# Norms of queries and keys summed in four quarters of the array, with square buffers kept for four chunks

## The chip, the cores and the metric

The kernel runs on one core of a Trainium2 chip. The metric is the device time of one execution in microseconds, as the median of several runs. The engines have an instruction stream each: TensorE (PE) multiplies matrices into PSUM, VectorE (DVE), ScalarE (ACT) and GpSimd (POOL) work on tiles, and SyncE (SP) and POOL issue DMA transfers. They wait for each other by semaphores only.

## What is computed

One layer over 4096 tokens of width 256: a layer norm, self-attention with 16 heads of 16, a shared expert and eight routed experts (two chosen for each token), all added to the input.

```python
xn = _layernorm(x)                                     # 4096 x 256
q, k, v = xn @ Wq.T, xn @ Wk.T, xn @ Wv.T              # 16 heads of 16
attn = softmax(einsum('bqhd,bkhd->bhqk', q, k) / 16)
att = einsum('bhqk,bkhd->bqhd', attn, v)
scores = softmax(xn @ gate_w.T); top 2 of scores + gate_b -> rw
h = silu((xn @ w1 + b1) * (xn @ w3 + b3))              # eight experts, width 352
x + att + sum_e rw * (h @ w2 + b2) + the shared expert
```

The softmax doesn't look for the largest energy of each row. It takes |q| max|k| as a bound: an exponent of q.k minus |q| max|k| is never positive. So the kernel needs |q| of each token and head and the largest |k| of each head. The product minus |q| max|k|, split into a high and a low part, is "the shift": two more rows of the contraction of each score matmul.

## The kernel before

**Two parts.** The front (0 to some 101 us) makes the layer norm, the projections of queries, keys and values, the norms and the shifts. The main loop (from the first score matmul to the end) goes over 16 heads and two sweeps of 2048 queries: PE makes scores (L863), ACT takes the exponential (L1157), PE multiplies by the values (L876), and the experts' matmuls (L888, L900) are woven in. The order of all instructions is written out by hand in each engine's function; nothing is planned by a scheduler.

**The front on PE.** Tokens go by eight chunks of 512 (`c`, NCH = 8, FIRST = 4). `turn_xn(c)` turns a chunk (L671), `keys(c, i)` and `queries(c, i)` project it with six matmuls of 128x512 each (L695, L696, L699), `late_queries` does so for chunks 4 to 7 at the end, and `value_rows(n)` makes values of two tiles with twelve matmuls (L764 to L766). ACT copies each projection out of PSUM and makes its squares in bf16 (`split_keys` L1057 and L1058, `split_queries` L1072 and L1073), and DVE takes the low part (`key_rest` L1322, `query_rest` L1329).

**The norms.** `key_norms(c)` (L727) and `query_norms(c)` (L736) sum the squares of one chunk over the 16 columns of each head: two matmuls of 128x128 with 512 moving columns, whose stationary operand is a slice of `hones_b` that puts the sums of chunk c on PSUM rows 16c to 16c+15. One buffer `sq` holds the squares of one chunk of keys and one of queries; ACT waits for the norms of chunk c-1 (`s_nk`, `s_nq`) before it writes those of chunk c. Keys add up in bank 7, queries of chunks 0 to 3 in rows 0 to 63 of bank 6, and those of 4 to 7 in rows 64 to 127 of bank 5.

**From norms to scores.** DVE reduces bank 7 (L1382), PE turns it (L803), DVE takes the largest per head (L1385), PE spreads it (L808), ACT takes the root (L1126). Then DVE makes the shifts of the first half of the queries from `qnorm` (`shift_rows(0)`, L1398 and L1400, 64 rows of 512), POOL stores them to DRAM (`store_shift`, L432, two transfers of 64 rows, 128 KB each), waits until both have landed (`s_sst[0]`), and loads the rows of head 0 into `q_ring` (`load_q_shift`, L424, four transfers that raise `s_qfirst`). PE's first score matmul waits for `s_qfirst` and for ACT's copies of the values (`s_vc`, L1081). The second half (queries 4 to 7) is made by L1133, `shift_rows(1)` and a store on SP. ACT's seventh exponential waits for both stores, because `qnorm` and `spart` lie in the buffer of `probs`.

**Queues.** POOL's transfers go by queue q0 of the DMA engines, those of SP by q1, where the stores of keys and queries are (`store_keys` L482, `store_queries` L489, 512 KB each).

Of the kernel before, what the change touches and what calls it, by code (L numbers as in the profile page):

```python
# [5 lines left out]
T = 4096  # L6
D = 256
# [138 lines left out]
def layer_program(nc, x, wqT, wkT, wvT, gT, gate_b, w1, w3, w2, b13, b2, ident, hones, prefix, ones, steps_c, out):  # L146
# [11 lines left out]
    with ctx:  # L158
# [7 lines left out]
        qshift_parts = nc.dram_tensor("qshift_parts", (NP_, H, T), f32, kind="Internal").ap()  # L166
# [7 lines left out]
        hones_b = sb("hones_b", [P, DT, 2 * P - H], bf16)  # L174
# [20 lines left out]
        o_n = sb("o_n", [P, NB_, HD], f32)  # L195
# [3 lines left out]
        zeros = sb("zeros", [P, TPU * D], f32)  # L199
        places_sb = sb("places_sb", [P, 3 * NT * E], f32)  # L200
# [47 lines left out]
        sq = pflat[:, 2048:3072].bitcast(bf16).rearrange("p (w i n) -> p w i n", w=2, i=DT)  # L248
# [170 lines left out]
        def load_q_shift(queue, h, sweep, landed):  # L419

            for r in range(2):
                for i in range(2):
                    dst = q_ring[r * HALF + SHIFT:r * HALF + SHIFT + NP_, sweep, i * QC:(i + 1) * QC].bitcast(f32)
                    queue.dma_start(dst, shift_cols[:, ds(h, 1), sweep, :, i, r, :].rearrange("s h c n -> (s h) c n")).then_inc(landed, 16)  # L424

        def store_shift(queue, half):

            rows = slice(half * HALF, (half + 1) * HALF)
# [9 lines left out]
        def _(sp):  # L438
# [71 lines left out]
            with sp.If(flag):  # L510
# [19 lines left out]
                for n in range(NCH):  # L530
                    sp.wait_ge(s_shift, n + 1)
                    sp.dma_start(qshift_parts[:, :, n * QC:(n + 1) * QC].rearrange("s h t -> h s t"), spart[0:H].bitcast(f32)).then_inc(s_gst, 16)
# [110 lines left out]
        def _(pe):  # L643
# [78 lines left out]
            def key_norms(c):  # L722

                pe.wait_ge(s_sq, key_job(c) + DT)
                own = slice(P - H - H * c, 2 * P - H - H * c)
                for dt in range(DT):
                    last = pe.matmul(bank(7), hones_b[:, dt, own], sq[:, 1, dt, :],  # L727
                                     start=(c == 0 and dt == 0), stop=(c == NCH - 1 and dt == DT - 1))
                last.then_inc(s_nk, 1)

            def query_norms(c):

                pe.wait_ge(s_sq, query_job(c) + DT)
                own = slice(P - H - H * c, 2 * P - H - H * c)
                for dt in range(DT):
                    last = pe.matmul(bank(6 if c < FIRST else 5), hones_b[:, dt, own], sq[:, 0, dt, :],  # L736
# [1074 lines left out]
```

## Time and profile before

| | us |
|---|---|
| median of 3 runs (lowest to highest) | 2132.31 (2130.73 to 2132.53) |
| the profiled execution, its own time | 2134.93 |
| its span | 2132.9 |
| PE busy | 2111.6 (99%) |
| ACT busy | 2016.2 (95%) |
| DVE busy | 805.7 (38%) |
| granted TensorE clock, as a share of full | 0.998 |

The span is the time from the first to the last instruction of the profiled execution; 2.0 us of its own time lie around it, and the median of the runs is 2.6 us below that time. Busy shares are means over two parts with different limits. Rows of the timeline give the start, the duration, the engine and line, and in brackets the idle time before the instruction and what ended it.

### The profile page before, as it was taken

The page shows a single profiled execution, that of the slowest core. Times are in us where ns is not written, and L with a number is a line of the kernel's source. Part 1 is how long each engine was busy: PE and PEld are TensorE (multiplying, and loading weights), DVE is VectorE, ACT ScalarE, POOL GpSimd, SP SyncE. Part 2 cuts the span into 40 slices and gives each one's busy share as a digit, 9 for nine tenths or more (in the row PEclk, how much of TensorE's full clock was granted, in tenths as well). Part 3 has the DMA queues.
Part 4 walks back from the last instruction along what each step waited for, and adds up shares of the span by engine and source line. Part 5 has one row for each costly group of instructions (what it writes and reads, how often), then busy time and mean ns, then how long its engine had stood idle before and what let it go on. Part 6 is the DMA issues. An engine that isn't in the chain of part 4 may idle for free.

```text
span 2132.9 us, 38290 instructions
## 1 busy us (share of the span) xinstructions
PE 2111.6 (99%) x15722; PEld 969.2 (45%) x15722; DVE 805.7 (38%) x1558; ACT 2016.2 (95%) x2228; POOL 253.5 (12%) x260
## 2 busy tenths in 40 slices
PE   8999999999999999999999999999999999999998
PEld 5734444444444444444444444444444444444442
DVE  7554333333333333333333333333333322244531
ACT  6699999999999999999999999999999999999998
POOL 0307764000000000000000000000000000122230
PEclk9999999999999999999999999999999999999999
DMA  8774433222231313132222221313122221322321
GB/s 284 263 251 126 125 123 100 60 53 72 58 79 51 76 52 82 51 78 60 64 59 72 63 75 51 87 44 79 51 79 59 71 68 57 85 80 86 105 91 41
DMA packets 223310, 187.28 MB, mean 88 GB/s; under 512 B 110623, under 2 KB 192342, under 8 KB 223134
## 3 DMA queue, kind: packets, MB, share of 16 engines
q1 hardware_dynamic: 209454, 148.68, 24.5%
q0 software_dynamic: 12624, 36.08, 5.2%
q8 instruction: 124, 2.03, 0.4%
q14 instruction: 52, 0.43, 0.1%
q10 hardware_dynamic: 1056, 0.07, 0.0%
HBM read 130.21 MB, written 54.53 MB: 87 GB/s over the span
## 4 chain that ended last, share of the span: by engine, by line
PE 95%; ACT 4%; DVE 1%; DMA 0%; issue 0%; SPq 0%; DVEq 0%; ACTq 0%
PE PS L876 44%; PE PS L863 31%; PE PS L888 12%; PE PS L900 6%; ACT probs L1157 3%; PE PS L695 0%; PE PS L696 0%; PE PS L699 0%; DMA hones_sb<-in_hones 0%; PE PS L764 0%; DVE probs L1303 0%; PE PS L671 0%; ACT x_parts L1038 0%; ACT x_full L1039 0%; PE PS L766 0%
## 5 line engine op out<-in xcount | busy, mean ns | idle before, releaser
L1157 ACT ACTIVATE probs<-PS 128x1024 f32<-128x1024 f32 x2048 | 1921.1, 1038 | 73.8 <-PE PS L863 45.1
L876 PE MATMUL PS<-probs,v_head 128*32 128x512 f32 x8192 | 989.9, 599 | 1.0 <-ACT probs L1157 0.8
L863 PE MATMUL PS<-q_ring,k_stack 50*128 50x512 f32 x4096 | 729.6, 443 | 5.7 <-ACT probs L1157 4.4
L863 PEld LDWEIGHTS PS<-q_ring,k_stack 50*128 50x128 f32 x4096 | 332.3, 184 | 607.4 <-ACT probs L1157 544.2
L876 PEld LDWEIGHTS PS<-probs,v_head 128*32 128x32 f32 x8192 | 211.4, 108 | 448.5 <-issue 372.9
L1598 DVE TENSOR_SCALAR gate_in<-PS,bias_sb 128x256 f32<-128x256 f32 (+7 forms) x165 | 76.4, 463 | 605.5 <-PE PS L888 597.0
L888 PE MATMUL PS<-x_hi,w_hi 128*128 128x256 f32 (+9 forms) x660 | 199.3, 302 | 0.0
L1227 POOL DMA_DIRECT2D slot_y<-y_sb x39 | 27.9, 716 | 1411.2 <-DVE y_sb L1668 1374.8
L888 PE MATMUL PS<-x_hi,w_lo 128*128 128x256 f32 (+9 forms) x660 | 184.9, 280 | 0.0
L888 PE MATMUL PS<-x_lo,w_hi 128*128 128x256 f32 (+9 forms) x660 | 184.2, 279 | 0.0
L888 PEld LDWEIGHTS PS<-x_hi,w_hi 128*128 128x128 f32 (+1 forms) x660 | 118.7, 180 | 53.2 <-issue 53.2
L888 PEld LDWEIGHTS PS<-x_lo,w_hi 128*128 128x128 f32 (+1 forms) x660 | 118.9, 180 | 0.0
L888 PEld LDWEIGHTS PS<-x_hi,w_lo 128*128 128x128 f32 (+1 forms) x660 | 118.9, 180 | 0.0
L1668 DVE COPY y_sb<-PS 128x512 f32<-128x512 f32 x39 | 27.0, 692 | 222.7 <-PE PS L900 222.7
L1608 DVE SCALAR_TENSOR_TENSOR hid<-hid,prod 128x768 f32<-128x768 f32 (+7 forms) x55 | 49.9, 908 | 130.1 <-ACT hid L1143 130.1
L900 PE MATMUL PS<-w_hi,hid_hi 128*128 128x256 f32 (+4 forms) x318 | 95.5, 300 | 0.0
L1629 DVE TENSOR_TENSOR w_lo<-w_raw,w_hi 128x1408 fp32r<-128x1408 f32 x55 | 89.2, 1622 | 1.6
L900 PE MATMUL PS<-w_lo,hid_hi 128*128 128x256 f32 (+4 forms) x318 | 89.6, 282 | 0.0
L900 PE MATMUL PS<-w_hi,hid_lo 128*128 128x256 f32 (+4 forms) x318 | 89.4, 281 | 0.0
L1218 POOL DMA_INDIRECT slot_x<-y_sb,pos x64 | 78.7, 1230 | 19.1 <-issue 14.0
L1603 DVE SCALAR_TENSOR_TENSOR prod<-PS,bias_sb,gate_in 128x256 f32<-128x256 f32 (+7 forms) x165 | 76.9, 466 | 5.9
L900 PEld LDWEIGHTS PS<-w_hi,hid_hi 128*128 128x128 f32 (+4 forms) x318 | 59.1, 186 | 13.4 <-issue 13.4
(186 smaller groups left out, 1148.7 us busy)
## 6 DMA issues: line engine op xcount, KB each, us to landing
w_raw<-in_w SPq DMA_DIRECT2D x110, 352.0 KB
k_stack<-qk_parts SPq DMA_DIRECT2D x120, 128.0 KB
w_raw<-in_w SPq DMA_DIRECT2D x55, 256.0 KB
q_ring<-qk_parts SPq DMA_DIRECT2D x372, 32.0 KB
qk_parts<-part_a SPq DMA_DIRECT2D x20, 512.0 KB, 4.3
slot_x<-zeros SPq DMA_DIRECT2D x39, 256.0 KB, 3.7
slot_in<-slot_x SPq DMA_DIRECT2D x156, 64.0 KB, 2.4
slot_y<-y_sb POOLq DMA_DIRECT2D x39, 256.0 KB, 2.5
```

The source lines that it names most:

```text
L863: last = pe.matmul(bank(2 * score_buffer(turn, g) + r), k_stack[rows, kt * P:(kt + 1) * P], q_ring[rows, sweep, i * QC:(i + 1) * QC], star ...
L876: last = pe.matmul(bank(O_BANK)[VW * j:VW * (j + 1), :], v_head[:, kt, :], probs[:, slot, (j % 2) * QC:(j % 2 + 1) * QC], start=(kt == 0), ...
L888: last = pe.matmul(f_half(w)[0:FT[j], 0:width(u)], a[u % 2][:, w, dt, j * P:j * P + FT[j]], b[:, dt * CH:dt * CH + width(u)], start=(n == ...
L900: last = pe.matmul(f_half(t)[0:own, :], a[0:rows, j, t * P:t * P + own], b[0:rows, j, :], start=(n == 0), stop=(n == 8))
L1157: nc.scalar.activation(probs[:, prob_slot(g), :], bank(2 * score_buffer(h, g), 2), ACT.Exp, scale=ENERGY_SCALE).then_inc(s_exp, 1)
L1218: nc.gpsimd.indirect_dma_start(out=slot_x, out_offset=bass.IndirectOffsetOnAxis(ap=pos[:, u * TPU + t, k:k + 1], axis=0), in_=rows[:, t, : ...
L1227: nc.gpsimd.dma_start(slot_y[(u - SA) * CH:(u - SA + 1) * CH, :].rearrange("(t p) d -> p t d", p=P), y_sb[:, u % 2, :].rearrange("p (t d) ...
L1598: V.tensor_scalar(gate_in[0:FT[j], 0:width(u)], f_half(0)[0:FT[j], 0:width(u)], bias_sb[0:FT[j], u % 2, j:j + 1], 0.5, ALU.add, ALU.mult). ...
L1603: V.scalar_tensor_tensor(prod[u % 2][0:FT[j], j, 0:width(u)], f_half(1)[0:FT[j], 0:width(u)], bias_sb[0:FT[j], u % 2, 3 + j:4 + j], gate_i ...
L1608: V.scalar_tensor_tensor(hid[:, :, 0:width(u)], hid[:, :, 0:width(u)], 1.0, prod[u % 2][:, :, 0:width(u)], ALU.add, ALU.mult).then_inc(s_h ...
L1629: V.tensor_tensor(w13_lo[u % 2][:, :, :, :], w13_raw[:, :, :, :], w13_hi[u % 2][:, :, :, :].bitcast(f32), ALU.subtract).then_inc(s_w13, 1)
L1668: V.tensor_copy(y_sb[:, u % 2, :], bank(F_BANK)).then_inc(s_yc, 1)
```

## The change

Buffers for the squares of four chunks of keys and four of queries replace `sq`. They lie in buffers that are free in the front (`o_t`, `x_t`, a part of `v_all`, and `early_sq`, into which `zeros`, `places_sb` and `o_n` are moved too). The norms are summed for four chunks at once: for each of the two halves of the width, four matmuls of 32 output columns, one for each chunk, to PSUM rows 32c to 32c+31. A half of a sequence has 16 valid rows in each quarter (keys of chunks 0 to 3 on the lower 16, of 4 to 7 on the upper 16 of each quarter, in one bank), the other 16 rows of a query bank are zero. So there are four blocks of eight matmuls in place of 16 pairs. ACT waits for norms twice in place of 14 times. `qnorm`, `spart` and the shift stores have 128 rows in place of 64 for each half (256 KB for each transfer), half of them zeros, and `load_q_shift` reads row sweep*H + h. Since both halves use the same rows of `qnorm` and `spart`, DVE takes the largest norm of the first half before its shifts (a new reduction), ACT's second root waits for the first shifts (`s_s1`), and `shift_rows(1)` waits for the first stores (`s_sst[0]`). POOL's `memset` of `zeros` waits for the last query norms.

```diff
-        hones_b = sb("hones_b", [P, DT, 2 * P - H], bf16)
+        hones_b = sb("hones_b", [P, DT, 3 * H], bf16)
...
-        sq = pflat[:, 2048:3072].bitcast(bf16).rearrange("p (w i n) -> p w i n", w=2, i=DT)
...
+        key_sq, query_sq = ([buf.bitcast(bf16).rearrange("p (i n) -> p i n", i=DT) for buf in bufs] for bufs in (
+            (pflat[:, 2048:2560], pflat[:, 2560:3072], o_t[:, :, :].rearrange("p b d -> p (b d)"), x_t[:, :]),
+            (early_sq[:, 0:QC], early_sq[:, QC:2 * QC], early_sq[:, 2 * QC:3 * QC], v_all[:, 22:24, :].rearrange("p t n -> p (t n)")[:, 0:QC])))
...
-                    queue.dma_start(dst, shift_cols[:, ds(h, 1), sweep, :, i, r, :].rearrange("s h c n -> (s h) c n")).then_inc(landed, 16)
+                    queue.dma_start(dst, shift_cols[:, ds(sweep * H + h, 1), sweep, :, i, r, :].rearrange("s h c n -> (s h) c n")).then_inc(landed, 16)
...
-                queue.dma_start(qshift_parts[s, :, cols].rearrange("h (c t) -> c h t", c=FIRST), spart[rows, s, :].bitcast(f32)).then_inc(s_sst[half], 16)
+                queue.dma_start(qshift_parts[s, :, cols].rearrange("h (c t) -> c h t", c=FIRST), spart[:, s, :].bitcast(f32)).then_inc(s_sst[half], 16)
...
+            def norms(w, half, b):
+
+                own = slice(0, 2 * H) if half else slice(H, 3 * H)
                 for dt in range(DT):
...
+                    for c in range(QCH):
+                        last = pe.matmul(bank(b)[2 * H * c:2 * H * (c + 1), :], hones_b[:, dt, own], (key_sq if w else query_sq)[c][:, dt, :],
+                                         start=((half == 0 or w == 0) and dt == 0), stop=((half == 1 or w == 0) and dt == DT - 1))
...
-            pe.wait_ge(s_hb, 2)
-            key_norms(0)
             for c in range(1, FIRST):
                 keys(c, 0)
-                query_norms(c - 1)
...
-                key_norms(c)
+                if c == FIRST - 1:
+                    pe.wait_ge(s_hb, 2)
+                    key_norms(0)
...
                 if c == FIRST:
-                    query_norms(FIRST - 1)
+                    query_norms(0)
...
-                key_norms(c)
+                if c == NCH - 1:
+                    key_norms(1)
...
-            query_norms(4)
...
-            query_norms(5)
...
-            query_norms(6)
...
-            query_norms(7)
+            query_norms(1)
...
-                if i == 0 and c:
-                    act.wait_ge(s_nq, c)
+                if i == 0 and c == FIRST:
+                    act.wait_ge(s_nq, 1)
...
+            act.wait_ge(s_nq, 2)
+            act.wait_ge(s_s1, NP_)
+            nc.scalar.activation(qnorm, bank(5), ACT.Sqrt).then_inc(s_qn, 1)
...
+            pool.wait_ge(s_nq, 2)
             nc.gpsimd.memset(zeros[:, :], 0.0).then_inc(s_zero, 1)
...
+                if half:
+                    dve.wait_ge(s_sst[0], 16 * NP_)
+                else:
+                    link(V.reduce_max(kmax[:, 3:4], qnorm, axis=AX))
+                V.tensor_scalar(spart[:, 0, :], qnorm, kmax[:, 2:3], None, ALU.mult).then_inc(s_s1, 1)
```

On PE, at the end of chunk 7 (the last key norms), the rows before are these; `probs` holds the squares:

```order
L766 MATMUL PS<-wvg_hi,x_parts 128x264
L727 MATMUL PS<-probs,hones_b 128x512 x2
L695 MATMUL PS<-x_parts,wqk_hi 128x512
L696 MATMUL PS<-x_parts,wqk_lo 128x512
L695 MATMUL PS<-x_parts,wqk_hi 128x512
```

and now, at the same place, the squares being in `probs`, `o_t` and `x_t`:

```order
L769 MATMUL PS<-wvg_hi,x_parts 128x264
L729 MATMUL PS<-probs,hones_b 32x512 x2
L729 MATMUL PS<-o_t,hones_b 32x512
L729 MATMUL PS<-x_t,hones_b 32x512
L729 MATMUL PS<-probs,hones_b 32x512 x2
L729 MATMUL PS<-o_t,hones_b 32x512
L729 MATMUL PS<-x_t,hones_b 32x512
L697 MATMUL PS<-x_parts,wqk_hi 128x512
```

Eight matmuls of 32 columns stand where a pair of 128 columns stood, and the pairs after chunks 4, 5 and 6 are gone.

On DVE, around the shifts of the first half, the rows before are

```order
L1329 TENSOR_TENSOR part_q<-PS,part_q 128x512 x2
L1392 TENSOR_SCALAR kmax<-kmax 128x1
L1398 TENSOR_SCALAR probs<-probs,kmax 64x512
L1400 SCALAR_TENSOR_TENSOR probs<-probs,kmax 64x512
L1329 TENSOR_TENSOR part_a<-PS,part_a 128x512 x4
```

and now

```order
L1331 TENSOR_TENSOR part_q<-PS,part_q 128x512 x2
L1394 TENSOR_SCALAR kmax<-kmax 128x1
L1402 TENSOR_REDUCE kmax<-probs 128x1
L1403 TENSOR_SCALAR probs<-probs,kmax 128x512
L1405 SCALAR_TENSOR_TENSOR probs<-probs,kmax 128x512
L1331 TENSOR_TENSOR part_a<-PS,part_a 128x512 x4
```

The reduction into `kmax` is new and stands ahead of both shift instructions, which have 128 rows; the low parts of chunks 6 and 7 follow as before.

## Rows read from the trace of the kernel before

**Rows 1.** Page: chain by engine, and the costliest group (busy us, mean ns | idle)

```profile
PE 95%; ACT 4%; DVE 1%; DMA 0%; issue 0%; SPq 0%; DVEq 0%; ACTq 0%
...
L1157 ACT ACTIVATE probs<-PS 128x1024 f32<-128x1024 f32 x2048 | 1921.1, 1038 | 73.8 <-PE PS L863 45.1
```

**Rows 2.** Chain of waits, in order of time: start us, us, engine and line

```profile
84.28 0.45 PE PS L736 x2
...
100.07 0.62 ACT v_all L1081
100.86 0.96 PE PS L863 x6
...
107.94 0.43 PE PS L863 x2
108.37 1.00 PE PS L876 x8
...
146.29 1.85 PE PS L876 x16
148.14 0.90 PE PS L863 x6
```

**Rows 3.** Timeline of PE in the front: start, us, line, shapes, [idle <-releaser]

```profile
1.46 6.55 PE L650 MATMUL PS<-o_t 128*128 128x512 bf16 x20 [1.46 <-DVE o_t L1273]
...
27.03 1.09 PE L671 MATMUL PS<-ident_sb,probs 128*128 128x128 f32 x8 [1.50 <-DVE probs L1303]
...
49.46 1.09 PE L671 MATMUL PS<-ident_sb,probs 128*128 128x128 f32 x8 [0.35 <-DVE probs L1303]
...
52.71 0.39 PE L764 MATMUL PS<-wvg_hi,x_parts 128*128 128x264 f32 x1 [0.30 <-ACT x_full L1039]
...
64.21 1.09 PE L671 MATMUL PS<-ident_sb,probs 128*128 128x128 f32 x8 [0.85 <-DVE probs L1303]
...
68.44 0.60 PE L727 MATMUL PS<-probs,hones_b 128*128 128x512 bf16 x2 [0.28 <-ACT probs L1058]
...
70.46 1.09 PE L671 MATMUL PS<-ident_sb,probs 128*128 128x128 f32 x8
...
74.69 0.60 PE L727 MATMUL PS<-probs,hones_b 128*128 128x512 bf16 x2 [0.28 <-ACT probs L1058]
...
94.46 0.61 PE L736 MATMUL PS<-probs,hones_b 128*128 128x512 bf16 x2
```

**Rows 4.** Timeline of DVE around chunk 7 and the shifts of the first half

```profile
69.03 1.37 DVE L1303 TENSOR_SCALAR probs<-resid,mv,rstd 128x256 f32<-128x256 f32 x4
...
88.08 0.48 DVE L1398 TENSOR_SCALAR probs<-probs,kmax 64x512 fp32r<-64x512 f32 x1
88.59 0.74 DVE L1400 SCALAR_TENSOR_TENSOR probs<-probs,kmax 64x512 fp32r<-64x512 f32 x1
...
95.91 0.69 DVE L1409 TENSOR_REDUCE qbound<-probs 128x1 f32<-128x512 f32 x1 [0.92 <-ACT probs L1133]
```

**Rows 5.** Timeline of POOL: the shift stores and the shift loads

```profile
88.85 1.41 POOL L432 DMA_DIRECT2D qshift_parts<-probs  x2 [3.22 <-DVE probs L1398]
95.55 2.20 POOL L424 DMA_DIRECT2D q_ring<-qshift_parts  x4 [5.29 <-DMA qshift_parts<-probs]
```

**Rows 6.** DMA issues at 88.8, 90 and 97.1 us: KB each, us to landing

```profile
qshift_parts<-probs POOLq DMA_DIRECT2D x1, 128.0 KB, 3.2
...
qshift_parts<-probs POOLq DMA_DIRECT2D x1, 128.0 KB, 5.6
...
q_ring<-qshift_parts POOLq DMA_DIRECT2D x2, 4.0 KB, 3.5
```

**Rows 7.** Window 81:91 (last: DMA share, GB/s); queues in 91:94: packets, MB, share

```profile
81.00:91.00 10.00, 10.00 (x45) 7.20 (x43) 5.14 (x10) 6.56 (x13) 5.93 (x12) 1.00 1.04 394
...
q1 hardware_dynamic: 354, 0.68, 61.1%
q0 software_dynamic: 246, 0.26, 40.2%
```

More of the change, by code:

```diff
@@ L198, in layer_program @@
         qbound = sb("qbound", [P, 2], f32)
-        zeros = sb("zeros", [P, TPU * D], f32)
-        places_sb = sb("places_sb", [P, 3 * NT * E], f32)
+        early_sq = sb("early_sq", [P, 3 * QC], f32)
         flag_f = sb("flag_f", [1, 4], f32)
@@ L720, in late_queries, with key_norms, query_norms @@
                 project(c, 0, i, late_bank(m))
-            def key_norms(c):
-                pe.wait_ge(s_sq, key_job(c) + DT)
-                own = slice(P - H - H * c, 2 * P - H - H * c)
+            def norms(w, half, b):
+                own = slice(0, 2 * H) if half else slice(H, 3 * H)
                 for dt in range(DT):
[L727 to L736, printed above, removed]
-                                     start=(c % FIRST == 0 and dt == 0), stop=(c % FIRST == FIRST - 1 and dt == DT - 1))
-                last.then_inc(s_nq, 1)
+                    for c in range(QCH):
+                        last = pe.matmul(bank(b)[2 * H * c:2 * H * (c + 1), :], hones_b[:, dt, own], (key_sq if w else query_sq)[c][:, dt, :],
+                                         start=((half == 0 or w == 0) and dt == 0), stop=((half == 1 or w == 0) and dt == DT - 1))
+                return last
+            def key_norms(half):
+                pe.wait_ge(s_sq, key_job((half + 1) * QCH - 1) + DT)
+                norms(1, half, 7).then_inc(s_nk, 1)
+            def query_norms(half):
+                pe.wait_ge(s_sq, query_job((half + 1) * QCH - 1) + DT)
+                norms(0, half, 6 - half).then_inc(s_nq, 1)
             def value_rows(n):
@@ L1057, in split_keys @@
                 nc.scalar.activation(key_part[c % 2][:, 0, i, :], bank(b), ACT.Copy).then_inc(s_hi, 1)
-                nc.scalar.activation(sq[:, 1, i, :], bank(b), ACT.Square).then_inc(s_sq, 1)
+                nc.scalar.activation(key_sq[c % QCH][:, i, :], bank(b), ACT.Square).then_inc(s_sq, 1)
             def split_queries(c, i):
@@ L1067, in split_queries @@
                     act.wait_ge(s_kst[0], stored(6))
-                if i == 0 and c:
-                    act.wait_ge(s_nq, c)
+                if i == 0 and c == FIRST:
+                    act.wait_ge(s_nq, 1)
                 b = 4 + i if c < FIRST else late_bank((c - FIRST) * DT + i)
@@ L1072, in split_queries @@
                 nc.scalar.activation(query_part[c][:, 0, i, :], bank(b), ACT.Copy).then_inc(s_hi, 1)
-                nc.scalar.activation(sq[:, 0, i, :], bank(b), ACT.Square).then_inc(s_sq, 1)
+                nc.scalar.activation(query_sq[c % QCH][:, i, :], bank(b), ACT.Square).then_inc(s_sq, 1)
             def keep_values(n):
@@ L1117, in _ @@
                     root(5)
-                    act.wait_ge(s_nq, FIRST)
-                    nc.scalar.activation(qnorm[0:HALF, :], bank(6)[0:HALF, :], ACT.Sqrt).then_inc(s_qn, 1)
+                    act.wait_ge(s_nq, 1)
+                    nc.scalar.activation(qnorm, bank(6), ACT.Sqrt).then_inc(s_qn, 1)
                 keep_values(c + 2)
@@ L1394, in shift_rows @@
             def shift_rows(half):
-                rows = slice(half * HALF, (half + 1) * HALF)
                 dve.wait_ge(s_qn, half + 1)
-                V.tensor_scalar(spart[rows, 0, :], qnorm[rows, :], kmax[rows, 2:3], None, ALU.mult).then_inc(s_s1, 1)
+                if half:
[3 more added lines that the diff above has]
+                V.tensor_scalar(spart[:, 0, :], qnorm, kmax[:, 2:3], None, ALU.mult).then_inc(s_s1, 1)
                 dve.wait_ge(s_s1, NP_ * half + 1)
-                V.scalar_tensor_tensor(spart[rows, 1, :], qnorm[rows, :], kmax[rows, 2:3], spart[rows, 0, :].bitcast(f32),
+                V.scalar_tensor_tensor(spart[:, 1, :], qnorm, kmax[:, 2:3], spart[:, 0, :].bitcast(f32),
                                        ALU.mult, ALU.subtract).then_inc(s_s1, 1)
@@ L1422, in _ @@
                 dve.wait_ge(s_tr, NCH)
-                dve.wait_ge(s_nk, NCH)
+                dve.wait_ge(s_nk, 2)
                 dve.wait_ge(s_kst[1], stored(NCH - 1))
```

19 lines of the change are left out of this document (9 added, 10 removed).

## The prediction

> **What bounds the kernel now.** I read the page first: 95% of the chain that ends last is PE, and its costliest partner, the exponentials of 1.04 us, keep pace beside it [rows 1]. The change touches nothing in that main loop, so it can only move the moment at which the loop starts. Read the chain of waits next, around 100 us: the first score matmul starts at 100.86, and the row before it is ACT's copy of the last values, which ends at 100.69 [rows 2]. That names PE's own work (norms, projections, values, then the copy) as what comes last. But the first score has a second condition, the shift rows of head 0. Read POOL's timeline for it: POOL stores the shifts from 88.85 on, sits idle for 5.29 us until both stores have landed, and issues four loads from 95.55 to 97.75 [rows 5]. The last load is issued at about 97.2 and such a load takes 3.5 us to land [rows 6], so the rows are there at about 100.7. Two chains thus end within 0.1 us of each other: PE's work, which the change shortens, and the way of the shifts through DRAM, which it loads with twice the bytes. The reader is to see this tie; all else hangs on it.
>
> **The cost of a block.** A pair of old norm matmuls takes 0.45 us [rows 2]; 16 pairs are 7.2 us of PE. No row shows bf16 matmuls of 32 columns, but the value matmuls have that shape: eight take 1.00 and sixteen 1.85 [rows 2], so each further four cost 0.43, and 0.14 is fixed. One full fp32 matmul of 512 columns would be two passes of the 0.225 that one old norm matmul takes, so four of them in 0.43 run side by side. In bf16 with one pass I take half, 0.215 for four, 0.43 for a block of eight. To that comes the change of shape, at both ends: 0.14 on entry as above, and on leaving it two score matmuls take 0.43 and six take 0.90 [rows 2], 0.235 for each pair and 0.20 fixed. A block is 0.43 + 0.14 + 0.20 = 0.77 us. Below, if the switches overlapped, it is 0.43; above, if the quarters don't overlap, 8 x 0.225 + 0.34 = 2.14. I take 0.77, since the value rows are the same shape with the same eight instructions. Four blocks are 3.1 us, so 4.1 us of PE's work go. How much of it is on the path?
>
> **Walk along PE.** At 27.03 PE sat idle 1.50 us for the layer norm on DVE [rows 3], so what is saved before is lost. From there to 49.46 one pair is on the path (queries of chunk 1), the others stand ahead of waits for ACT or DVE: -0.45. The first key block (0.77 in place of 0.45) stands ahead of 0.30 us idle at 52.71 [rows 3], which covers it. The first query block costs +0.32 in the open. That makes -0.13 at the turn of chunk 6 at 64.21, where PE is idle 0.85 for DVE, whose own work came after keys that moved by this -0.13. At 68.44 the pair of chunk 5 goes, and with it 0.28 us of waiting for its square and the refilling behind it, 0.88 in all; but the turn of chunk 7 at 70.46 needs DVE's last normalise, which ends at 69.03 + 1.37 = 70.40 [rows 3, 4], so this gain is lost but for the 0.13. At 74.69 the same 0.88 goes and nothing waits behind: -1.01. The second key block adds 0.32: -0.69. The pair of queries of chunk 4 goes: -1.14 when the largest key norm is known. The pairs of chunks 5 and 6 go: -2.04. The last query block adds 0.32, partly hidden (the last values wait for DVE anyway), so values and their copies end about 1.85 earlier. PE alone would allow the first score at 100.86 - 1.85 = 99.0.
>
> **Walk along the shifts.** DVE's shifts start at 88.08 [rows 4] and move by -1.14, as the root does. Ahead of them stands the new reduction over 128x512, 0.69 in the row of its twin [rows 4], with its link 0.72. So they end 0.42 earlier. With 128 rows for 64 the instructions on DVE keep their time, as the same columns pass. The stores are issued 0.42 earlier and carry 0.26 MB more together. No row shows them; the nearest ones are the stores of half the size, which landed 3.2 and 5.6 us after issue [rows 6], while the DMA engines were full: from 81 to 91 us the share is 1.04 at 394 GB/s [rows 7]. Three prices. At the full rate, 0.26 MB / 394 GB/s = 0.66 us. At the share that POOL's queue had while it moved such rows, 40.2% [rows 7], it is 1.66. At the rate it then reached, 0.26 MB in 3 us [rows 7], it is 3.0. I take 1.66: SP's stores of chunks 6 and 7 are issued 1 to 2 us earlier too, so they meet the shift stores. The stores then land 1.66 - 0.42 = 1.24 later, POOL's four loads follow 1.24 later, and the rows of head 0 are there at 101.9. The first score starts 1.2 us later than before: the path of the shifts decides, and PE's gain is idle time of some 3.9 us before it.
>
> The row shows 40.2% for POOL's queue. The Trainium skill, DMA: Bandwidth & Descriptors, section Queues, rings and completion order, says that each DMA engine goes round its queues by packets, which gives two full queues half each. With that the extra bytes would be an estimated 1.3 us in place of 1.66, and the time 0.3 us less; the row is a little worse than the rule.
>
> **Edits at no cost.** The roots on ACT take the same columns. The buffers of the squares are free memory. ACT's fewer waits let it run ahead, but PE waits for none of its squares but the last. The new reduction delays the low part of chunk 6, on which the last projections wait, to about the moment they need it: 0.1 at most, in the slack of PE. POOL's `memset` waits for norms that are done when POOL comes to it after its loads; SP needs the zeros only behind all its loads of keys and queries. `shift_rows(1)` waits for the stores of the first half (96.4 or so), when its flag chain ends anyway; behind it on DVE stand the copies of head 0's values, which need ACT's copies first. The second half's stores are issued by 98.5; at 5.6 us [rows 6] and 1.7 more they land before 106, and ACT's seventh exponential comes six exponentials of 1.04 [rows 1] after 102.1. If that cover were gone, ACT would stall for the difference, and PE with it.
>
> **The sum.** -0.42 + 1.66 = +1.24. The profiled execution took 2134.93 with a span of 2132.9, and would take 2136.2; the median of the runs is 2132.31 and becomes 2133.5.
>
> **Rivals.**
> 1. *The bytes hide.* The engines have gaps, and the stores may fill them at the full rate: +0.66 - 0.42 = +0.2; if 128 rows cost nothing, -0.4. About 2132.3. For it: a store of 64 rows is a few packets for each DMA engine. Against it: the full engines [rows 7]. The time a DMA takes may be mostly fixed: the Trainium skill, DMA: Bandwidth & Descriptors, section Anatomy of one DMA, gives 2.0 us fixed and the bytes at 436 GB/s. By that the larger stores cost an estimated 0.6 us more, which is this case; the row of 5.6 us for 128 KB speaks against an empty queue.
> 2. *PE's chain decides.* If the shifts were ready before PE, the whole -1.85 arrives: 2130.5. It needs the stores to land 1.4 us earlier than they are issued earlier, so only a lucky order of packets gives it.
> 3. *The quarters don't overlap.* Each block is 2.14. The walk gives -1.01 + 1.69 - 0.45 = +0.23 at the key norms, so the stores are issued 0.95 later and land 2.6 later: 2134.9. Against it: the value matmuls overlap [rows 2]. This is also the case in which the change doesn't do what it says.
> 4. *PE cools down while it waits* (slower). If the stores cost the upper price, the first score starts 3.0 - 0.42 = 2.6 later and PE stands idle 4.5 us. After an idle time its granted clock may be the lower of its two levels (1.2 for 2.4 GHz): the first 20 matmuls of the kernel, after nothing, take 6.55 us [rows 3] where 20 x 0.225 = 4.5 would do, 2.05 lost. Together +4.65: 2137.0. Against it: the gap of 2 us between the first matmuls and the first turn left no trace of this. It decides from an idle time somewhere over that, which no row gives.
>
> **How the numbers follow.** The forecast (shifts decide, +0.3 to +2.6) has 0.50, the bytes that hide 0.22, PE's chain 0.10, no overlap 0.08, the cooled PE 0.05, anything unforeseen 0.05. The likeliest time is 2133.5. The range from 2130.5 to 2135.0 holds the forecast, the first three rivals and leaves out the cooled PE and the unforeseen, with the scatter of the median (1.8 us between the runs) at its edges. 0.2% is 4.3 us, about what a measurement of this kernel can tell from no change. Only the cooled PE and half of the unforeseen are slower by that; faster by that would need 4.1 us, all of PE's saving, on the path: 0.02. Slower 0.06, same 0.92.
>
> **What would show it.** In the profile after: blocks of eight matmuls of 32 columns that cost the stream about 0.77 us; the chain around 64 and 70 us still held by DVE's normalise; the last key block some 0.7 to 1.0 us early. POOL's wait between its shift stores and its loads longer than 5.29, near 7.0. The first score at 102, its releaser the shift loads and no more ACT's copy, PE idle for more than 3 us before it. A first score at 99 would refute the price of the stores; one at 101 with a POOL wait of 5.7 would be the bytes that hide; a block over 1.5 us the quarters; score matmuls at 0.45 us each right after the gap the clock. From the first score to the end the span should be as before, 2032.0 us; if that changes by more than 0.5, my view that the loop doesn't feel the change is wrong.

## Result and the profile after

| | before | after |
|---|---|---|
| median of 6 runs, us | 2132.42 (2130.73 to 2132.90) | 2143.56 (2141.01 to 2146.75) |
| ratio to before | | 1.0051 (95% interval 1.0042 to 1.0061) |
| span of the profiled execution, us | 2132.9 | 2144.9 (of a run of 2146.75) |
| first score matmul, us | 100.86 | 111.34 |
| first value matmul, us | 106.88 | 119.31 |
| from there to the end, us | 2026.0 | 2025.6 |

The forecast was 2133.5, with a range from 2130.5 to 2135.0. The kernel became 11.1 us slower by the medians. The profiled execution after is the slowest of its six, so between the two profiles the difference is 12.0 us of span. It is all there by 119.31 us; behind that the two kernels take the same time. Page of the kernel after, to set against [rows 1]: the page's section 5 (busy us, mean ns | idle us and what ended most of it).

```profile
L1158 ACT ACTIVATE probs<-PS 128x1024 f32<-128x1024 f32 x2048 | 1921.2, 1037 | 87.6 <-PE PS L863 58.5
...
L863 PE MATMUL PS<-q_ring,k_stack 50*128 50x512 f32 x4096 | 729.6, 443 | 18.2 <-DMA q_ring<-qshift_parts 13.4
```

The exponentials take the same 1921 us. But ACT now waits 58.5 us for score matmuls where it waited 45.1, and the score matmuls wait 13.4 us in one piece, for the shift loads. Chain of waits after, the stretch of [rows 2] (start us, us, what):

```profile
84.34 0.48 PE PS L701 x2
84.84 0.60 ACT part_q L1072
85.44 0.50 ACT early_sq L1073
86.06 0.51 issue
86.75 0.69 DVE kmax L1402
87.47 0.50 DVE probs L1403
88.25 0.73 POOL qshift_parts L434
89.03 11.37 DMA qshift_parts<-probs
100.69 1.60 POOL q_ring L427 x3
102.33 8.93 DMA q_ring<-qshift_parts
111.34 1.65 PE PS L863 x6
```

PE is gone from the chain at 84.8 us. From 88 to 111 us the chain is the way of the shifts through DRAM and back: one store that lands 11.4 us after its issue, then one load of 4 KB that lands after 8.9. In [rows 6] the same two took 5.6 and 3.5. The first score is 10.48 us later. That adds up: the stores are issued 0.60 earlier (88.25 for 88.85), POOL waits 10.95 us for them and not 5.29, its four loads so begin 5.14 later, and the last load takes 5.4 longer. Timeline of POOL after, to set against [rows 5], and below it SP's DMA issues in the same stretch:

```profile
88.25 1.49 POOL L434 DMA_DIRECT2D qshift_parts<-probs  x2 [2.86 <-DVE probs L1403]
100.69 2.20 POOL L427 DMA_DIRECT2D q_ring<-qshift_parts  x4 [10.95 <-DMA qshift_parts<-probs]
```

```profile
88.78 6.91 SPq L491 DMA_DIRECT2D qk_parts<-part_a  x4
101.01 1.33 SPq L434 DMA_DIRECT2D qshift_parts<-probs  x2
102.39 0.74 SPq L465 DMA_DIRECT2D k_stack<-qk_parts  x1
```

SP issues the second half's stores at 101.01, beside POOL's loads; in the kernel before it issued them at 98.5. They are late because DVE's second shifts now wait for the first stores to land (`shift_rows(1)`). DVE stands 4.58 us before them, where the kernel before made them at 98.00:

```profile
100.50 0.48 DVE L1403 TENSOR_SCALAR probs<-probs,kmax 128x512 fp32r<-128x512 f32 x1 [4.58 <-DMA qshift_parts<-probs]
```

Windows after (PE, PEld, DVE, ACT and POOL busy us, PE's granted clock, DMA share, GB/s):

```profile
91.00:94.00 3.00, 3.00 (x29) 2.43 (x28) 1.36 (x3) 2.51 (x5) 0.00 (x0) 1.00 0.96 257
...
100.00:105.00 5.00, 0.00 (x0) 0.00 (x0) 1.74 (x5) 0.00 (x0) 3.92 (x8) 0.71 0.25 68
105.00:110.00 5.00, 0.00 (x0) 0.00 (x0) 0.00 (x0) 0.00 (x0) 0.61 (x1) 0.50 0.53 162
110.00:115.00 5.00, 3.65 (x15) 2.97 (x16) 0.00 (x0) 2.82 (x3) 0.00 (x0) 0.50 0.34 109
```

Two things are to be seen. From 100 to 105 us, with the second half's 512 KB of shift stores issued from 101.01 on and little else moving, the DMA engines are busy to 0.25: a quarter of sixteen, at 68 GB/s. There the path is slow although the engines are mostly idle. And the granted clock falls to 0.50, its level of 1.2 GHz, after PE has stood idle from about 98: from the first score to the first values it takes 7.97 us (before 6.02), so 1.95 us come on top of the 10.48.

PE's own part went as the change meant it. Timeline of PE after, against [rows 3]: the last key block, the turns of chunks 6 and 7, and then, from ACT's timeline, the last value copy (before 100.07):

```profile
78.28 0.39 PE L729 MATMUL PS<-probs,hones_b 128*32 128x512 bf16 x2
78.29 0.39 PE L729 MATMUL PS<-o_t,hones_b 128*32 128x512 bf16 x1
78.29 0.39 PE L729 MATMUL PS<-x_t,hones_b 128*32 128x512 bf16 x1
78.51 0.38 PE L729 MATMUL PS<-probs,hones_b 128*32 128x512 bf16 x2
```

```profile
63.94 1.09 PE L673 MATMUL PS<-ident_sb,probs 128*128 128x128 f32 x8 [1.30 <-DVE probs L1305]
```

```profile
70.18 0.98 PE L673 MATMUL PS<-ident_sb,probs 128*128 128x128 f32 x7 [0.91 <-DVE probs L1305]
```

```profile
98.03 0.61 ACT L1081 ACTIVATE v_all<-PS 128x528 f32<-128x528 f32 x1 [0.79 <-PE PS L769]
```

Four quarter matmuls start within 0.01 us of each other and the next four 0.23 us later; the next projection starts 0.55 us after the first of the block. (In the kernel before it started 0.26 us after the first of the pair, at 79.62 for 79.36, so the block costs 0.29 us more than the pair.) Both turns are held by DVE, and the last values are copied 2.04 us earlier. None of it reaches the end.

### The profile page after: what moved, and what is told of

Its sections match the earlier page's. It is cut to its first block, busy times and chain, and to the rows that moved or that the text cites. A ratio compares the mean times of both kernels' runs of the same rounds, so it can differ in the third digit from the quotient of the medians.

```text
span 2144.9 us, 38292 instructions
## 1 busy us (share of the span) xinstructions
PE 2110.0 (98%) x15722; PEld 969.8 (45%) x15722; DVE 806.6 (38%) x1559; ACT 2016.4 (94%) x2228; POOL 253.9 (12%) x260
## 4 chain that ended last, share of the span: by engine, by line
PE 93%; ACT 3%; DMA 1%; DVE 1%; issue 0%; POOL 0%; SPq 0%; another core or an unknown queue 0%; DVEq 0%; ACTq 0%
PE PS L876 43%; PE PS L863 30%; PE PS L888 12%; PE PS L900 6%; ACT probs L1158 3%; DMA qshift_parts<-probs 1%; DMA q_ring<-qshift_parts 0%; PE PS L673 0%; DVE probs L1305 0%; PE PS L697 0%; PE PS L698 0%; PE PS L701 0%; DMA hones_sb<-in_hones 0%; PE PS L767 0%; PE PS L768 0%
## 5 line engine op out<-in xcount | busy, mean ns | idle before, releaser
L1158 ACT ACTIVATE probs<-PS 128x1024 f32<-128x1024 f32 x2048 | 1921.2, 1037 | 87.6 <-PE PS L863 58.5
L863 PE MATMUL PS<-q_ring,k_stack 50*128 50x512 f32 x4096 | 729.6, 443 | 18.2 <-DMA q_ring<-qshift_parts 13.4
```

The lines of the kernel that those rows point to most:

```text
L863: last = pe.matmul(bank(2 * score_buffer(turn, g) + r), k_stack[rows, kt * P:(kt + 1) * P], q_ring[rows, sweep, i * QC:(i + 1) * QC], star ...
L1158: nc.scalar.activation(probs[:, prob_slot(g), :], bank(2 * score_buffer(h, g), 2), ACT.Exp, scale=ENERGY_SCALE).then_inc(s_exp, 1)
```

## The experiments

**Theory.** Three parts. *Few engines*: each shift store, written to DRAM with an outer dimension of 4 (the chunks), runs on 4 of the 16 DMA engines. So twice the bytes cost twice the time of a few engines, and 2 MB of query stores on the DMA engines beside them (four stores of 512 KB) delay them further. *Wait*: the new wait of `shift_rows(1)` moves the second half's stores from ahead of POOL's loads to beside them. *Clock*: the idle PE falls to the lower level. Rivals: the bytes cost what 16 engines take; scattered rows in DRAM are slow; the new norms or their order are the cause.

The share of 0.25 is this case's evidence for the first part. The Trainium skill, DMA: Bandwidth & Descriptors, section Why a DMA increments its semaphore by 16 and not by 1, has the rule: the number of engines is the largest one up to 16 that divides the slowest dimension of both sides. Here that is 4, for the store of before (4x16x512) as for that of after (4x32x512), and the trace agrees with it where the second half's stores are nearly alone (0.25 here, and 0.27 at 66 GB/s from 108 to 110 us in e3_hold below).

For POOL's stores of the first half "few engines" is not the whole account. What its queue q0 moved from 91 to 94 us, as a share of the time of sixteen engines, and beside it the share and rate of all queues:

| kernel | POOL's stores | q0: MB | q0: share | all: share, GB/s |
|---|---|---|---|---|
| after | two of 256 KB, outer dimension 4 | 0.24 | 37.8% | 0.96, 257 |
| e1_spread | two of 256 KB, 128 whole rows | 0.31 | 26.4% | 1.03, 390 |
| e6_before_twice | four of 128 KB, outer dimension 4 | 0.32 | 71.7% | 0.95, 194 |

A share of 37.8% is the time of six engines and 71.7% that of more than eleven; [rows 7] had 40.2% before, with all engines together at 1.04. So it is unlikely that the two stores of a half lay on one and the same quarter. And a busy engine moved less in this form: 37.8% for 0.24 MB against 26.4% for 0.31 MB is 1.9 times the engine time for each byte. All queues together show it too, in the last column. The runs below show that the outer dimension makes these stores slow; how much of that is the number of engines, and how much the fewer bytes for each busy one, they don't tell apart.

The table has all runs; "ratio" is to runs of the kernel before on the same chip. All times but the ratio are of the one profiled execution, in us.

| kernel | last first-half store, issue to landing | POOL's loads from | first score | first values | ratio (95% interval) |
|---|---|---|---|---|---|
| before | 5.6 | 95.55 | 100.86 | 106.88 | |
| after | 11.4 | 100.69 | 111.34 | 119.31 | 1.0051 (1.0042 to 1.0061) |
| e1_spread | 6.3 | 95.43 | 100.80 | 108.31 | 1.0008 (0.9998 to 1.0018) |
| e2_chunks | 6.9 | 99.64 | 103.48 | 112.17 | 1.0021 (1.0012 to 1.0031) |
| e3_hold | 12.5 | 101.38 | 105.22 | 113.82 | 2138.74, one run (before 2128.57) |
| e4_warm | 11.2 | 100.42 | 110.60 | 116.63 | 1.0041 (1.0027 to 1.0055) |
| e5_before_spread | 3.9 | 93.83 | 100.80 | 106.82 | 0.9993 (0.9983 to 1.0002) |
| e6_before_twice | 8.5 | 99.42 | 107.54 | 115.83 | 1.0040 (1.0024 to 1.0055) |
| e8_eight | 6.9 | 95.31 | 102.54 | 110.52 | 1.0021 (1.0012 to 1.0031) |
| e7_best | 6.3 | 93.90 | 99.65 | 105.66 | 0.9994 (0.9985 to 1.0003) |
| e9_order | 5.9 | 93.22 | 99.84 | 108.37 | 0.9999 (0.9990 to 1.0008) |

The moment of the first values explains the totals. Its distance from 106.88, divided by the time before, lies within the interval of the ratio for each kernel with one: e6 8.95 us or 1.0042, e4 9.75 or 1.0046, e1 1.43 or 1.0007, e7 -1.22 or 0.9994. (For the kernel after it is 12.43 us or 1.0058.)

### The same bytes as whole rows (e1_spread)

```diff
-        qshift_parts = nc.dram_tensor("qshift_parts", (NP_, 2 * H, T), f32, kind="Internal").ap()
+        qshift_parts = nc.dram_tensor("qshift_parts", (NP_, 2, P, QC), f32, kind="Internal").ap()
...
-                queue.dma_start(qshift_parts[s, :, cols].rearrange("h (c t) -> c h t", c=FIRST), spart[:, s, :].bitcast(f32)).then_inc(s_sst[half], 16)
+                queue.dma_start(qshift_parts[s, half], spart[:, s, :].bitcast(f32)).then_inc(s_sst[half], 16)
```

> The changed kernel, but the shift rows lie in DRAM as 128 rows of 512 (chunk, head) for each half, so that each store is a plain 128x512 transfer; bytes and rows of 2 KB as in the changed kernel. Theory F (few engines): in the changed kernel the outermost dimension of the store's DRAM side is 4 (its pattern is 4x32x512), and such a store runs on only 4 of the 16 DMA engines; 64 KB for each of four engines at 24.6 GB/s (394 / 16) are 2.7 us for a store, 5.3 beside a full second queue, and 5.5 and 11.4 were measured. Spread over 16 engines both stores should land within 3 to 4.5 us of issue, the loads be issued at about 92.5, and the last one land by 97; PE then decides: first score at 98.9, PE idle under 1 us before it, no fall of the granted clock, time 2130.5 (2129.8 to 2131.5), 13 us less than the changed kernel. Rival B (the bytes): twice the bytes on full DMA engines cost what they cost however they are spread: landing still over 9 us after issue, first score after 108, time over 2140. Rival W (the new wait of the second shifts for the first stores): it would shrink with the landing only, so under B it stays.

POOL's timeline in e1_spread:

```profile
88.08 0.58 POOL L433 DMA_DIRECT2D qshift_parts<-probs  x1 [2.91 <-DVE probs L1402]
88.87 0.56 POOL L433 DMA_DIRECT2D qshift_parts<-probs  x1 [0.21 <-issue]
95.43 2.22 POOL L427 DMA_DIRECT2D q_ring<-qshift_parts  x4 [6.00 <-DMA qshift_parts<-probs]
```

One layout in DRAM takes 10.5 us off the first score with every byte, norm and wait of the change kept (the loads read the rows at their new places), and the last load is back at 3.6 us. So the bytes themselves cost little. Two forecasts missed, the landing (3 to 4.5 us) and the first score (98.9): the store still takes 6.3 us beside the query stores, so PE still waits 2.97 us for the shift rows and does not decide, and its clock falls (below).

### The same addresses in four stores (e2_chunks)

```diff
-                queue.dma_start(qshift_parts[s, :, cols].rearrange("h (c t) -> c h t", c=FIRST), spart[:, s, :].bitcast(f32)).then_inc(s_sst[half], 16)
+                for c in range(FIRST):
+                    queue.dma_start(qshift_parts[s, :, (half * FIRST + c) * QC:(half * FIRST + c + 1) * QC], spart[2 * H * c:2 * H * (c + 1), s, :].bitcast(f32)).then_inc(s_sst[half], 16)
```

> The changed kernel with its DRAM layout and addresses kept, but each shift store issued as four transfers of 32 rows (one for each chunk), so 16 engines can take part; the same bytes in 8 issues. It tells the number of engines from the DRAM addresses, which the run with 128 contiguous rows changes too. Theory F: POOL's eight issues take 8 x 0.7 = 5.6 us from 88.25, so the last is issued at about 93.2 and lands 3 to 4 later, at 96.5 to 97; loads from 97 to 99, the last lands at 102 (or 103 if the second stores are in its way): 8 to 9 us before the changed kernel's 111.2, time 2132 to 2135. If the addresses (rows 16 KB apart) or the bytes were the cause, landing stays near 11 us after issue, or later with eight issues, time 2143 or more.

The rows go to the same scattered places as in the kernel after, but each store has 32 rows on both sides. The first score comes at 103.48, 7.9 us earlier, although POOL now needs 3.95 us to issue eight stores (last one at 92.5, landing after 6.9). So scattered rows are not what cost the 10 us. (These stores still land after 6.9 us beside the query stores, and PE idles 4.67 us.)

### Eight in place of four (e8_eight)

```diff
-        qshift_parts = nc.dram_tensor("qshift_parts", (NP_, 2 * H, T), f32, kind="Internal").ap()
+        qshift_parts = nc.dram_tensor("qshift_parts", (NP_, 2, 8, 17, QC), f32, kind="Internal").ap()
...
-                queue.dma_start(qshift_parts[s, :, cols].rearrange("h (c t) -> c h t", c=FIRST), spart[:, s, :].bitcast(f32)).then_inc(s_sst[half], 16)
+                queue.dma_start(qshift_parts[s, half, :, 0:16], spart[:, s, :].bitcast(f32)).then_inc(s_sst[half], 16)
```

> The kernel after, with the shifts laid out in DRAM as 8 blocks of 16 rows with one unused row behind each: the store has an outer dimension of 8. Theory (the outer dimension sets the number of engines): 8 engines, so between after and e1_spread: DMA share up to 0.5 while POOL waits, last store landing 6.3 to 8 us after issue (after 11.4, 16 engines 6.3), first score at 101 to 103.5, total 2 to 5 us above the kernel before. Rival (what e1_spread cured was long strides or the scattered rows, and any layout of whole contiguous rows is as good): exactly as e1_spread, first score 100.8, total 2 us above before. Rival (only a wholly contiguous store is fast): as in after, first score near 111.

Chain of waits in e8_eight:

```profile
88.09 6.94 DMA qshift_parts<-probs
95.31 1.60 POOL q_ring L427 x3
96.95 5.50 DMA q_ring<-qshift_parts
102.54 1.65 PE PS L862 x6
```

All between the two: store 6.9 (11.4 and 6.3), last load 5.5 (8.9 and 3.6), first score 102.54 (111.34 and 100.80). As in e1_spread whole rows lie together, but for one unused row behind each 16; what differs is the outer dimension. From 128 rows in one piece to eight pieces the first score moves by 1.7 us, although e8_eight issued its stores 0.78 us earlier; from eight to four it moves by 8.8, with the rows scattered as well, which e2_chunks has shown to matter little. So the outer dimension sets the time, and not in proportion: eight recover most of it. The DMA share doesn't single out eight engines here: it falls from 0.57 to 0.37 between 98 and 101 us, with loads of keys beside the stores.

### Twice the stores in the kernel before (e6_before_twice)

```diff
                 queue.dma_start(qshift_parts[s, :, cols].rearrange("h (c t) -> c h t", c=FIRST), spart[rows, s, :].bitcast(f32)).then_inc(s_sst[half], 16)
+                if half == 0:
+                    queue.dma_start(scratch[s, :, cols].rearrange("h (c t) -> c h t", c=FIRST), spart[rows, s, :].bitcast(f32)).then_inc(s_sst[half], 16)
...
-            pool.wait_ge(s_sst[0], 16 * NP_)
+            pool.wait_ge(s_sst[0], 16 * NP_ * 2)
```

> The kernel before, norms and all, but each first-half store of the shifts is issued twice, the second copy to a scratch tensor, and POOL waits for both: 512 KB in the same form with outer dimension 4, and nothing else of the change. Theory (few engines): DMA share at 0.3 or less while POOL waits, last store landing 9 to 12 us after issue, first score at 104 to 108, granted clock below 1 after it, total 5 to 8 us above the kernel before. Rival (the bytes cost what 16 engines take): first score near 102.1 and total 1 to 2 us above. Rival (what is slow in the kernel after comes from the new norms or the wait of shift_rows(1), not from the stores): total within 1 us of before.

POOL's timeline, and the window from 102 to 104 us, in e6_before_twice:

```profile
90.64 0.62 POOL L435 DMA_DIRECT2D scratch<-probs  x1
99.42 2.20 POOL L425 DMA_DIRECT2D q_ring<-qshift_parts  x4 [8.15 <-DMA scratch<-probs]
```

```profile
102.00:104.00 2.00, 0.00 (x0) 0.00 (x0) 0.00 (x0) 0.00 (x0) 1.68 (x3) 0.80 0.30 79
```

The old norms, the old order and no new wait: 0.26 MB more in the old form alone move the first score by 6.68 us and the median by 7.9. That is nearly three quarters of the whole loss, and it refutes the rival that sees the cause in the norms or in the new wait alone. The price that I gave these bytes was 1.66. The landing I expected at 9 to 12 us was 8.5; the rest of the delay lies behind it, as the first score comes 6.4 us after the issue of the last load at 101.1, with the second half's stores (from 98.4 on) beside it.

### Hold back the second half's stores (e3_hold)

```diff
+            sp.wait_ge(s_qfirst, HEAD_Q)
             store_shift(sp, 1)
```

> The changed kernel, but SP holds back the stores of the second half's shifts until the loads of head 0's shift rows have landed. Theory: in the changed kernel the second half's shifts wait for the first stores and are stored at 101.0 to 102.3, at the same moment as POOL's four loads (100.7 to 102.9), whose last one took 8.9 us to land where it took 3.5 before; two 256 KB stores on four engines lie in front of it there. With the stores held back the last load should land 3 to 4 us after issue, first score at about 106 and not at 111.3, time 5 us less than the changed kernel: 2138 to 2140. The first stores still land 11 us after issue. Rival: the load is slow for another reason (POOL's queue, DRAM): it still takes 8 to 9 us and the first score stays at 111.

Chain of waits in e3_hold:

```profile
88.60 12.49 DMA qshift_parts<-probs
101.09 0.28 issue
101.38 1.60 POOL q_ring L427 x3
103.02 2.12 DMA q_ring<-qshift_parts
105.15 0.61 SPq L434
105.81 10.71 DMA qshift_parts<-probs
116.59 1.94 ACT probs L1159 x2
```

With nothing beside it the same load of 4 KB lands in 2.1 us, not 8.9. So the second stores cost the loads 6.8 us, and the first score comes 6.1 earlier than in the kernel after. But the 512 KB that were held back then take 10.7 us, and ACT's seventh exponential waits 2.0 us for them: the wait that the prediction named as a cover is real once it is gone. (One run only, so this rests on the chain.)

### Keep PE busy (e4_warm)

```diff
+            for n in range(58):
+                pe.matmul(bank(7), blank[:, 0:P], blank[:, 0:QC], start=True, stop=True)
             pe.wait_ge(s_kone, 2)
```

> The changed kernel with 58 matmuls of 512 bf16 columns into an idle bank between the last value rows and the wait for the first score, 58 x 0.215 = 12.5 us of work, as in the warm-up at the start. The first score stays at 111.3 (the shift rows decide). Theory C (clock): in the changed kernel the granted clock was 0.50 of full from 105 to 115 after PE had been idle since 98, and the stretch from the first score to the first value matmuls took 8.0 us where it took 6.0 before. With PE kept busy the clock stays at 1.00, the stretch takes 6.0, the time is 2.0 us less: 2141.5. Rival: the clock costs nothing since the exponentials are the limit there: the time stays at 2143.5.

Chain of waits in e4_warm, and a window of it:

```profile
97.89 12.53 PE PS L824 x58
110.60 0.99 PE PS L865 x6
...
116.63 1.06 PE PS L878 x8
```

```profile
110.00:115.00 5.00, 4.62 (x31) 3.29 (x30) 0.71 (x1) 3.86 (x5) 0.00 (x0) 1.00 0.30 99
```

The granted clock stays at 1.00, six score matmuls take 0.99 and not 1.65, and first score to first values takes 6.03 us as in the kernel before (6.02), not 7.97. In the trace the clock is worth 1.9 us of the loss; what remains is the path of the shifts. (The intervals of the two ratios, 1.0041 and 1.0051, overlap, so this rests on the chain and not on the medians.)

### The kernel before with the better layout (e5_before_spread)

The edit of e1_spread, with 64 rows.

> The kernel before, with only the layout of the shifts in DRAM changed: 64 whole rows of 512 instead of columns of 16 long rows, so that its 128 KB stores have no outer dimension of 4. Theory (few engines): the stores can use all 16 DMA engines and land sooner than 5.6 us after issue (4 to 5 us, since the query stores still share the engines); POOL's loads go out 0.5 to 1.5 us earlier than 95.55, and PE's own chain, ready at 100.68, decides instead: first score 100.7, total 0 to 0.4 us below the kernel before. Rival (the layout does not matter, bytes alone do): landings and first score as in the kernel before (100.86).

POOL's loads go out at 93.83, 1.7 us earlier than before, and the first score stays at 100.80, behind ACT's last value copy: the slow layout cost the kernel before nothing, because PE's own chain ended at the same time. That is why the form of this store had not shown. Its two stores land after 3.8 and 3.9 us, where those of [rows 6] took 3.2 and 5.6 with the same bytes.

### Both put together (e7_best, e9_order)

e7_best is e1_spread with these two edits:

```diff
-                else:
-                    link(V.reduce_max(kmax[:, 3:4], qnorm, axis=AX))
...
             shift_rows(0)
+            V.reduce_max(kmax[:, 3:4], qnorm, axis=AX).then_inc(s_early, 1)
...
-            act.wait_ge(s_s1, NP_)
+            act.wait_ge(s_early, 1)
...
+            for n in range(9):
+                pe.matmul(bank(7), blank[:, 0:P], blank[:, 0:QC], start=True, stop=True)
             pe.wait_ge(s_kone, 2)
```

> e1_spread (16 engines) with two more edits: the maximum of the first half's norms is taken behind the two shift operations instead of ahead of them (0.69 us less ahead of the stores), and 9 matmuls without use (128x512) stand on PE ahead of its wait for the first score, so that its clock stays up. Theory: stores 0.7 us earlier than in e1_spread, first score at 100.1 instead of 100.8, granted clock 1.0 after it, first values at 106.1 to 106.3 (before 106.88, e1_spread 108.31), total 0.3 to 1.0 us below the kernel before. Rival (the shift path hangs on the query stores beside it, not on when its own stores start): first score stays at 100.8, total within 0.3 us of before. Rival (dummy matmuls come late and delay the scores): first score after 101.

Timeline of PE in e7_best, and a window of it:

```profile
99.65 0.96 PE L865 MATMUL PS<-q_ring,k_stack 50*128 50x512 f32 x6 [0.53 <-issue]
```

```profile
100.00:105.00 5.00, 4.79 (x36) 3.71 (x34) 0.81 (x2) 4.69 (x5) 0.00 (x0) 1.00 0.44 142
```

First score 99.65, first values 105.66: 1.2 us earlier than before, clock 1.00. The median is 2128.35 against 2129.62, a ratio of 0.9994 whose interval reaches 1.0003: better than the kernel after by far, and not separable from the kernel before. The mended change is worth 1 us or nothing.

e9_order takes the nine matmuls out again and lets SP wait for the first stores ahead of its last query stores:

```diff
             for c in range(FIRST, NCH):
+                if c == NCH - 1:
+                    sp.wait_ge(s_sst[0], 16 * NP_)
                 store_queries(c)
```

> e7_best without its 9 unused matmuls, and SP waits for the first half's shift stores before it issues the last 1 MB of query stores, so that the shift stores meet one query store on the DMA engines instead of two. Theory (what is left of the shift path is the queue beside it): shift stores land by 91.5 to 93 instead of 93.9, POOL's loads go out then and land before PE is ready, and PE's chain with ACT's last value copy decides: first score 98.0 to 98.6, no idle stretch long enough for the granted clock to fall (1.0), first values at 104.1 to 104.7 (e7_best 105.66), total 1 to 1.5 us below e7_best in span, that is 0.1% below the kernel before. Rival (the span from the first values on takes what was won, since the last query store lands later and later loads wait for it): first score as said and the same total as e7_best. Rival (the loads, not the stores, set it): first score stays at 99.6.

The forecast fell. The stores landed at about 93 and POOL's loads went out 0.7 us earlier than in e7_best, but the first score came at 99.84: it is the rival that the loads set it which fits. The last query stores (moved back) and the second half's stores from 95.01 on lie beside the loads; that these slow them is argued from the times and not shown by a run. The run shows the clock once more, at almost the same first score as e7_best: from there to the first values 8.53 us in place of 6.01, after 3.22 us of idle PE.

## Why the prediction was wrong

**The walk along PE: right.** I gave -1.01 ahead of the second key block and -0.69 behind it (measured -1.08, 78.28 for 79.36, and -0.79, 78.83 for 79.62), -1.85 at the end (measured -2.04), a block that costs 0.32 us more than a pair (0.29 at the next projection), and both turns held by DVE: so it was.

**The walk along the shifts up to the stores: right.** 0.42 earlier was 0.60. That the shift path takes over from PE was right too, and with it the sign.

**The price of the bytes: the step that failed.** "No row shows them; the nearest ones are the stores of half the size": I then priced the extra 0.26 MB at the full rate of the engines, at the share that POOL's queue had of them, and at the rate of that queue over a whole window: 0.66, 1.66 and 3.0 us. In this form they cost the store 5.8 us (11.4 for 5.6), and in e6_before_twice such bytes alone cost +6.7 at the first score. All three prices, and the 1.66 that I took, left out the form of the store. My own rows could have said so. [rows 6] has the first 128 KB store landing after 3.2 us and the second, issued 0.8 us later, after 5.6: the second adds 3.2 us for 128 KB, 41 GB/s, a tenth of the 394 GB/s of [rows 7]. I put the late landing down to the full engines. It was crowding and the form together: the same 128 KB as whole rows land after 3.9 us beside the same query stores (e5_before_spread). The `"h (c t) -> c h t"` that makes the shape 4x16x512 stood in the diff.

**"such a load takes 3.5 us to land": the second step that failed.** I carried it over unchanged. It took 8.9, since the second half's stores lay beside it. What put them there is the new wait, which the prediction named and costed at nothing, "`shift_rows(1)` waits for the stores of the first half (96.4 or so), when its flag chain ends anyway". A wait on a landing inherits every error in that landing: the stores landed at 100.4, the second stores moved from 98.5 to 101.0, next to the loads. In e3_hold the load is back at 2.1. These two terms, loads issued 5.1 us later (forecast 1.24) and the last one landing 5.4 us later after its issue (forecast 0), are the 10.5 us.

**The cooled PE: right in size, wrong in chance.** I gave 2.05 us from the first matmuls of the kernel and it cost 1.95 (e4_warm recovers 1.94), but I gave the case 0.05, as if only an idle time over that of my forecast could bring it. The forecast itself had 3.9 us of idle PE, and in e1_spread 2.97 us of idle already cost 1.5; before, 0.83 cost nothing. (The 4.5 us of rival 4 leave out the 0.83 that the 3.9 count.) So the forecast lacked this term even with its own price of the bytes.

**The main loop: right.** First values to the end is 2026.0 before and 2025.6 after. By the sign that the prediction set, first score to the end within 0.5 us of 2032.0, it would count as wrong: that stretch is 2033.6. The 1.5 us more lie ahead of the first values, in the slower clock.

**The range.** It rests on three prices that all left out the form of the store, so 0.66 to 3.0 looked wide and was not. A price from what the second store really added, 0.26 MB at 41 GB/s, is 6.4 us, near the 5.8 measured (in hindsight; after, the second store adds 6.7 us for 256 KB, 39 GB/s, so the rate held); it would have moved the range and most of the chance to the slower side.

## What to carry over

Before you price more bytes of a DMA, look at the outer dimension of its two sides: what an already slow transfer takes per byte is a better price than the rate of the full engines, and a layout of whole rows that lie together (128 and 64 of them in these runs) moves the same bytes. A new wait on a landing is priced from the late landing, together with the transfers that it moves beside others. A gain on one of two chains that end together is worth nothing until the other is shortened too; here the two were 0.1 us apart.

## What the runs showed of the hardware

- While 512 KB of stores with outer dimension 4 were under way almost alone, the DMA share was 0.25 at 68 GB/s (after, 100 to 105 us), and such stores landed after 10.7 us (e3_hold); the same stores as 128 whole rows landed 2.8 to 4.4 us after issue (e1_spread, e7_best, e9_order).
- Beside full queues a busy DMA engine moved fewer bytes when stores with outer dimension 4 were among its work: 257 GB/s at a share of 0.96 (after, 91 to 94 us) against 390 at 1.03 (e1_spread).
- A 4 KB load took 2.1 us beside nothing (e3_hold), 5.5 beside stores with outer dimension 8 (e8_eight) and 8.9 beside stores with outer dimension 4 (after). That a smaller outer dimension hurts the neighbour more I had not expected.
- Matmuls of 128x512 bf16 into 32 columns of four different quarters start within 0.01 us of each other, four per 0.23 us, about the time of one full one (0.225).
- After 2.97 us (e1_spread) and 3.22 us (e9_order) of idle PE its granted clock fell to 0.50 for a few us and cost 1.5 and 2.5 us up to the first values. After 13.4 us (after) it cost no more, 1.95, and after 4.67 (e2_chunks) 2.7; after 0.5 to 0.8 us (e7_best, before) nothing. In e7_best, with nine matmuls without use ahead of the first score, it stayed at 1.00.

Left open: the profile doesn't list the DMA engines one by one, so "4 of 16" is read from the share of the second half's stores, the times at 4, 8 and 128 rows, and the rule. How the first half's stores lie on the engines, and why a busy engine moves fewer bytes beside them, stays open. Why the spread store still takes 6 us beside the query stores was not settled; e9_order held the last 1 MB of these back and gained only 0.4.
